# Layer 1's experts hold gate and up weights in the array: products two and four tiles behind the rows, matches in fours

## The reference

```
scores = sigmoid(x @ gate_weight.T)            # 32 experts, biased, in groups; the top 6 of a token
g, u   = x @ w_gate[e], x @ w_up[e]            # 256 -> 128 each, for every chosen expert e
routed = sum over the 6 of  weight * (silu(g) * u) @ w_down[e]
ag, au = x @ anchor_w_gate[l], x @ anchor_w_up[l]   # 256 -> 64 each, one anchor l of 16 per token
anchor = (silu(ag) * au) @ anchor_w_down[l]
x      = x + routed + shared expert + 0.1 * anchor
```

## Time and profile before

| | us |
|---|---|
| median of 3 runs | 1128.87 |
| lowest, highest | 1126.39, 1144.8 |
| the profiled execution's own time | 1131.93 |
| its span, first to last instruction | 1130.2 |
| busy: PE, weight loads, DVE | 943.6, 690.6, 656.6 |
| busy: ACT, POOL | 481.3, 536.7 |

### The profile page before, as it was taken

How to read it: one execution, slowest core, us unless ns; L and a number is a source line. 1 busy time by engine, 2 the same in 40 slices (tenths; PEclk the granted TensorE clock), 3 DMA queues, 4 the chain that set the end, 5 groups by cost and what they waited for, 6 DMA issues and landing times. The chain is left out here.

```text
span 1130.2 us, 23159 instructions
## 1 busy us (share of the span) xinstructions
PE 943.6 (83%) x6360; PEld 690.6 (61%) x6360; DVE 656.6 (58%) x3235; ACT 481.3 (43%) x1594; POOL 536.7 (47%) x543
## 2 busy tenths in 40 slices
PE   5987888765799999969879989758799999998970
PEld 2665665544368889537657657544587777776740
DVE  3676566543135445456877677647465555555578
ACT  2875566443113333226555444221154444454520
POOL 1024555546414444599444344446465555545530
PEclk9998888766799999998987687568899999999965
DMA  9997311003459993465011141276668644444397
GB/s 332 345 371 260 108 59 46 30 10 116 155 172 317 316 317 118 190 237 210 2 67 67 57 174 72 77 290 235 228 206 247 186 144 137 142 136 130 89 366 263
DMA packets 114064, 198.53 MB, mean 176 GB/s; under 512 B 18712, under 2 KB 86381, under 8 KB 110866
## 3 DMA queue, kind: packets, MB, share of 16 engines
q1 hardware_dynamic: 83922, 138.27, 37.4%
q0 software_dynamic: 22944, 50.38, 12.1%
q10 hardware_dynamic: 7072, 8.40, 2.3%
HBM read 113.72 MB, written 98.72 MB: 188 GB/s over the span
## 5 line engine op out<-in xcount | busy, mean ns | idle before, releaser
L986 POOL DMA_INDIRECT buf<-R,RI x240 | 234.9, 979 | 306.5 <-ACT R L1134 158.2
L771 PE MATMUL PS<-R,XT 128*128 x632 | 155.5, 370 | 10.7 <-DVE XT L1598 10.1
L1022 POOL DMA_INDIRECT yb<-YT,DI x98 | 95.3, 973 | 112.8 <-DVE DI L1591 81.0
L315 PE MATMUL PS<-R 128*128 128x256 f32 (+2 forms) x352 | 125.8, 492 | 12.9 <-DMA R<-in_ctxT 10.1
L1598 DVE COPY XT<-PS 128x256 f32<-128x256 f32 x222 | 93.7, 422 | 71.7 <-PE PS L320 53.5
L771 PEld LDWEIGHTS PS<-R,XT 128*128 128x128 f32 x632 | 105.6, 196 | 22.3 <-issue 14.8
L787 PE MATMUL PS<-R,AT 128*128 (+1 forms) x316 | 102.1, 406 | 0.8 <-issue 0.6
L315 PEld LDWEIGHTS PS<-R 128*128 128x128 f32 (+1 forms) x352 | 72.8, 227 | 47.5 <-issue 37.0
L1134 ACT ACTIVATE R<-R,MX 128x120 f32<-128x120 f32 x256 | 80.0, 387 | 33.2 <-DVE MX L1424 21.9
L473 PE MATMUL PS<-C,R 128*120 128x128 f32 x512 | 83.6, 311 | 10.9 <-issue 10.7
L1142 ACT COPY R<-PS 120x512 f32<-120x512 f32 x96 | 54.7, 578 | 87.5 <-PE PS L473 46.3
(11 more groups left out here) (209 smaller groups left out, 1945.8 us busy)
## 6 DMA issues: line engine op xcount, KB each, us to landing
R<-in_ew SPq DMA_DIRECT2D x64, 384.0 KB
BX<-buf SPq DMA_DIRECT2D x128, 140.0 KB
yb<-Z SPq DMA_DIRECT2D x16, 1024.0 KB
R<-yb SPq DMA_DIRECT2D x16, 1024.0 KB, 4.8
R<-buf SPq DMA_DIRECT2D x94, 140.0 KB
R<-in_w SPq DMA_DIRECT2D x8, 1536.0 KB, 11.2
R<-yb SPq DMA_DIRECT2D x8, 1536.0 KB, 10.3
buf<-Z SPq DMA_DIRECT2D x8, 1120.0 KB, 13.5
```

The costliest lines, as they stand in the source:

```text
L315: m = e.matmul(out_, left, right, start=(i == 0), stop=(i == len(pairs) - 1))
L771: x = e.matmul(PS[:, 2 + j % 2, 0:2 * wd], XT[:, j % 3, k, :], src[:, bass.ds(regs[j], 1), k * 2 * wd:(k + 1) * 2 * wd].rearrange("p a n - ...
L986: e.indirect_dma_start(out=(buf1 if l else buf0)[:, :], out_offset=bass.IndirectOffsetOnAxis(ap=RI[:, n % 6, k:k + 1].bitcast(U32), axis=0 ...
L1022: e.indirect_dma_start(out=yb[:, :], out_offset=bass.IndirectOffsetOnAxis(ap=DI[:, j:j + 1].bitcast(U32), axis=0), in_=(YTS0 if i < E0 els ...
```

## The change

For layer 1's experts only:

- PE's gate and up product is turned round. ACT copies a tile's gate and up weights (128x512, or 128x256 for an anchor) from the resident weights, through a register, to one of two halves of `SS_`; PE takes 128x128 pieces of the copy as the stationary operand and streams the turned rows. A routed tile takes four products of 128 columns (each two passes), an anchor tile two, with gate and up side by side in one.
- The product comes out turned, so the transpose of `AC`, the copy to `AT` and their waits are gone; `AC1` (four slots) is the down product's stationary operand.
- The product runs two tiles behind the transposes and the down product four; before they ran one and three behind. Turned rows have three PSUM banks and four slots (`XT1`), products three banks.
- Rows are loaded into 8 slots (`RX`) that lie over H2T, so the first load waits for the last shared product that reads it.
- Matching is done once for four tiles, with four instructions, after all four have landed; a slot's next load waits for its batch. `TE` is written in the order of the tiles for it.
- PE, SP and now ACT load table entries by fours into registers, without the check of their bounds.

```diff
+        h2f = H2T[:, :, :].rearrange("p c n -> p (c n)")
+        RX = h2f[:, 0:NB1 * ROW].rearrange("p (s n) -> p s n", s=NB1)
+        XT1 = h2f[:, 2560:3584].rearrange("p (s c t) -> p s c t", s=4, c=2)
+        AC1 = h2f[:, 3584:4096].rearrange("p (s n) -> p s n", s=4)
+        XB, GB1 = (0, 1, 6), (2, 3, 7)
...
+            def of(self, i):
+                o = ORDER[i]
+                kind, first, size = (0, 0, T1) if o < T1 else (1, T1, TA)
+                b = (o - first) // 4
+                if (kind, b) not in self.had:
+                    at = first + 4 * b
+                    self.had.pop((kind, b - 2), None)
+                    self.had[kind, b] = nc.values_load_multi_w_load_instructions(
+                        self.table[0:1, at:min(at + 4, first + size)], engines=[self.engine], min_val=0,
...
+                return self.had[kind, b][(o - first) % 4]
...
-            for i in range(NTL + 3):
+            who, regs = Numbers(mybir.EngineType.PE, TI, R1 - 1, NA - 1), {}
+            for i in range(NTL + 4):
                 if i < NTL:
-                    regs[i] = e.value_load(TI[0:1, ORDER[i]:ORDER[i] + 1], min_val=0, max_val=(R1 if ORDER[i] < T1 else NA) - 1)
-                    turn_rows(E0 + i)
-                if 0 <= i - 1 < NTL:
...
-                    for k in range(2):
-                        x = e.matmul(PS[:, 2 + j % 2, 0:2 * wd], XT[:, j % 3, k, :],
-                                     src[:, bass.ds(regs[j], 1), k * 2 * wd:(k + 1) * 2 * wd].rearrange("p a n -> p (a n)"),
-                                     start=(k == 0), stop=(k == 1))
-                    x.then_inc(S["s_g"], 1)
+                    w.wait_ge(*landed(i))
+                    if i > 2:
+                        w.wait_ge("d_xt", E0 + i - 2)
+                    tr2(e, PS[:, XB[i % 3], 0:256], RX[:, i % NB1, 0:D]).then_inc(S["s_ta"], 1)
                 if 0 <= i - 2 < NTL:
                     j, wd = i - 2, width(i - 2)
+                    regs[j] = who.of(j)
+                    w.wait_ge("d_xt", E0 + j + 1)
+                    w.wait_ge("a_gu", j + 1)
+                    if j > 2:
+                        w.wait_ge("d_ac", E0 + j - 2)
+                    for o in range(2 if routed(j) else 1):
+                        x = mm(e, PS[:, GB1[j % 3], o * P:o * P + P],
+                               [(SS_[:, j % 2, 2 * wd * k + o * P:2 * wd * k + o * P + P], XT1[:, j % 4, k, :]) for k in range(2)])
+                    x.then_inc(S["s_g"], 1)
+                if 0 <= i - 4 < NTL:
+                    j, wd = i - 4, width(i - 4)
                     w.wait_ge("d_ac", E0 + j + 1)
                     if j > 1:
-                        w.wait_ge("a_at", j - 1)
-                    e.transpose(PS[0:wd, 6 + j % 2, 0:P], AC[:, j % 2, 0:wd], ident).then_inc(S["s_t2"], 1)
...
-                    e.matmul(PS[:, 4 + j % 2, 0:256], AT[0:wd, j % 2, :], src.rearrange("p a n -> p (a n)"),
+                    e.matmul(PS[:, 4 + j % 2, 0:256], AC1[0:wd, j % 4, :], src.rearrange("p a n -> p (a n)"),
                              start=True, stop=True).then_inc(S["s_y"], 1)
...
-                r = e.value_load(TU[0:1, ORDER[i]:ORDER[i] + 1], min_val=0, max_val=DUM_A)
+                r = units.of(i)
+                if i == 0:
+                    w.wait_ge("s_gu", 16 + 4)
...
+                if i >= NB1:
+                    w.wait_ge("s_ta", E0 + i - NB1 + 1)
+                    w.wait_ge("d_m", (i - NB1) // BATCH + 1)
...
+            def gate_copy(j):
+                src = (W1 if routed(j) else WA)[:, bass.ds(who.of(j), 1), 0:4 * width(j)]
+                w.wait_ge(*group_of(j))
+                e.copy(SS_[:, j % 2, 0:4 * width(j)], src.rearrange("p a n -> p (a n)")).then_inc(S["a_gu"], 1)
+
+            for i in range(NTL + 4):
...
+                if 0 <= i - 2 < NTL:
+                    j = i - 2
                     w.wait_ge("s_g", E0 + j + 1)
                     if j > 1:
                         w.wait_ge("d_ac", E0 + j - 1)
-                    e.activation(SL[:, j % 2, 0:wd], PS[:, 2 + j % 2, 0:wd], ACT.Silu).then_inc(S["a_sl"], 1)
...
-                    e.copy(AT[0:wd, j % 2, :], PS[0:wd, 6 + j % 2, 0:P]).then_inc(S["a_at"], 1)
...
+                if 0 <= i - 4 < NTL:
+                    yt_out(E0 + i - 4)
+                if i < NTL:
+                    gate_copy(i)
...
+            def matches1(i):
+
+                n, b = min(BATCH, NTL - i), i // BATCH
+                for k in range(i, i + n):
+                    w.wait_ge(*landed(k))
+                rows = RX[:, i % NB1:i % NB1 + n, :]
+                e.tensor_tensor(MEQ[:, 0:n, :], rows[:, :, 256:264], TE[:, i:i + n].unsqueeze(2).broadcast_to([P, n, 8]),
+                                ALU.is_equal).then_inc(*dv.up())
+                w.wait_ge("dv", dv.n)
+                e.tensor_tensor(MDW[:, 0:n, :, :], rows[:, :, 264:280].rearrange("p j (c k) -> p j c k", c=2),
+                                MEQ[:, 0:n, :].unsqueeze(2).broadcast_to([P, n, 2, 8]), ALU.mult).then_inc(*dv.up())
+                if b > 1:
+                    w.wait_ge("a_yt", E0 + BATCH * (b - 1))
+                w.wait_ge("dv", dv.n)
+                e.tensor_reduce(MS[:, b % 2, 0:n, :], MDW[:, 0:n, :, :], AX.X, ALU.add).then_inc(*dv.up())
+                w.wait_ge("dv", dv.n)
+                e.tensor_scalar(DI[:, i:i + n], MS[:, b % 2, 0:n, 0], OFF, None, ALU.add).then_inc(S["d_m"], 1)
...
+            for i in range(NTL + 4):
                 if i < NTL:
-                    xt_copy(E0 + i)
-                    w.wait_ge(f"bx{(E0 + i) % NBX}", 16 * ((E0 + i) // NBX + 1))
-                    matches(E0 + i, TE[:, ORDER[i]:ORDER[i] + 1])
-                if 0 <= i - 1 < NTL:
...
+                    e.tensor_copy(XT1[:, i % 4, :, :], two(PS[:, XB[i % 3], 0:256])).then_inc(S["d_xt"], 1)
+                    if i % BATCH == 0:
+                        matches1(i)
+                if 0 <= i - 2 < NTL:
+                    j = i - 2
                     w.wait_ge("a_sl", E0 + j + 1)
...
-                if ROUTED + 6 <= i:
-                    yf_add(i - ROUTED - 6)
+                if ROUTED + 7 <= i:
+                    yf_add(i - ROUTED - 7)
```

More of the change, by code:

```diff
@@ L32 @@
 NBX = 7
+NB1 = 8
+BATCH = 4
 NYT = 6
@@ L185, in build @@
         DI = sb("DI", [P, NTL], I32)
-        TE = sb("TE", [P, NTL])
+        TE = sb("TE", [P, NTL + 1])
         TI = sb("TI", [P, NTL], I32)
@@ L341, in all_back, with routed, landed, arrival @@
                 w.wait_ge(f"yt{s}", 16 * n)
+        def routed(i):
+            return ORDER[i] < T1
+        def landed(i):
+            s = i % NB1
+            return arrival(s), 16 * (i // NB1 + 1 + (len(range(s, E0, NBX)) if s < NBX else 0))
+        def arrival(s):
+            return f"bx{s}" if s < NBX else "rx7"
+        def group_of(i):
+            return (f"w1_{min(ORDER[i] // 4, 7)}", 16) if routed(i) else ("wa", 16 * 16)
+        class Numbers:
+            def __init__(self, engine, table, routed_most, anchor_most):
+                self.engine, self.table, self.most, self.had = engine, table, (routed_most, anchor_most), {}
+            def of(self, i):
[7 more added lines that the diff above has]
+                        self.table[0:1, at:min(at + 4, first + size)], engines=[self.engine], min_val=0,
+                        max_val=self.most[kind], skip_runtime_bounds_check_because="the table holds minima with this bound",
+                        bass_reorder=False)[1]
+                return self.had[kind, b][(o - first) % 4]
         def width(i):
@@ L1236, in yt_out @@
                 w.wait_ge("s_y", i + 1)
-                w.wait_ge("d_wc", i + 1)
+                if i < E0:
+                    w.wait_ge("d_wc", i + 1)
+                    weight = WC[:, j % 8:j % 8 + 1]
+                else:
+                    w.wait_ge("d_m", j // BATCH + 1)
+                    weight = MS[:, j // BATCH % 2, j % BATCH, 1:2]
                 slot, n = result(i)
@@ L1242, in yt_out @@
                     w.wait_ge("s_dn", 4 * EARLY if i < E0 else 32)
-                e.activation((YTS0 if i < E0 else YTS)[slot], PS[:, 4 + j % 2, 0:256], ACT.Copy, scale=WC[:, j % 8:j % 8 + 1]).then_inc(
+                e.activation((YTS0 if i < E0 else YTS)[slot], PS[:, 4 + j % 2, 0:256], ACT.Copy, scale=weight).then_inc(
                     S["a_yt"], 1)
@@ L1308, in _ @@
                         w.wait_ge("d_ac", E0 + j - 1)
[L1309 to L1317 removed]
+                    if routed(j):
+                        e.activation(SL[:, j % 2, :], PS[:, GB1[j % 3], 0:P], ACT.Silu).then_inc(S["a_sl"], 1)
+                    else:
+                        e.activation(SL[64:P, j % 2, :], PS[0:64, GB1[j % 3], 0:P], ACT.Silu).then_inc(S["a_sl"], 1)
+                if 0 <= i - 4 < NTL:
+                    yt_out(E0 + i - 4)
+                if i < NTL:
+                    gate_copy(i)
             for g in range(4):
@@ L1893, in _ @@
```

(17 more changed lines are left out.)

75 lines of the change are left out of this document (31 added, 44 removed).

## The result

The changed kernel took 1141.86 us (median of 4 runs, 1136.87 to 1147.64) beside 1133.69 for the kernel before in the same comparison: a ratio of 1.0129, 95% interval 1.0071 to 1.0187. The forecast was 1116 with a range of 1099 to 1139. The time moved the other way, by less than 2%. The profiled execution took 1136.87, its span 1135.2.

The account below looks back on a forecast made before the run. PE's instruction stream was taken to bound layer 1's expert stage, with 24.6 us of stalls besides. Products -10.2, anchors -2.1, start -1.0, drain +1.1 and tail -1.0 sum to -13.2: median some 1116 us, range 1099 to 1139.

Parts of the forecast that it names:

- Stalls: PE's stalls between tiles 3 and 146, 24.6 us before: no net change, 0, with both ends left open.
- over price: Tiles 3 to 146 should take 229.8 us by cost per tile; they took 254.4, the other 24.6 being stalls.
- the copies feel the stalls more: Rival, PE waiting for ACT at the product: some 30 times 0.45 us, +6 to +17 us; 15%.
- Products: PE's routed tiles in layer 1: 0.080 us less than 1.627 each over 127 tiles, -10.2 us.
- anchors: PE's anchor tiles: each loses the 0.11 us transpose, 19 ahead of the last routed tile, -2.1 us.
- The weight-load rule: Rival: four more weight loads lie bare in each routed tile, 4 x 0.196 us a tile, over 1200 us; 2%.
- The copy: ACT's new 128x512 weight copy from SBUF: 0.60 us, starting 1.0 after the product's end, hidden by throughput.
- Its slack: Hand-over of ACT's copy to PE through two buffers: 0.45 us of slack, so hidden.
- Register loads: Loads of four numbers on PE, SP and ACT: 0 taken; four in a row would cost +27 us.
- Start: PE's first transpose no longer waits behind a 0.86 us register load, which comes two tiles later: -1.0 us.
- Drain and tail: Last routed down product one anchor tile later, +1.1 us; four anchor tiles between DVE's final adds, not five, -1.0 us.
- The stalls go: Rival: fewer sequencer instructions and deeper queues remove half to nearly all of 24.6 us, giving 1091 to 1103; 22%.

Follow-up runs that it names:

- before, on time: Kernel before, unedited, in a group where PE's signals are not late: 989.24 us, tiles 3 to 146 in 233.5 us.
- changed, on time: Changed kernel, unedited, against the kernel before where PE's signals are not late: 983.51 us, ratio 0.9944.
- before, late: Kernel before, unedited, in a group where many of PE's signals come over 0.4 us late: 1133.69 us.
- changed, late: Changed kernel, unedited, against the kernel before where many of PE's signals come over 0.4 us late: 1141.86 us, ratio 1.0129.
- the copy ahead: Changed kernel with ACT's weight copy one tile further ahead, three buffers for two; against the kernel before 0.9877 with signals on time, 0.9998 with signals late.
- the two late groups: Unedited changed kernel against the kernel before, twice where PE's signals come late: 1141.86 us (1.0129) and 1137.67 us (1.0054).

## Why the prediction was wrong

Each piece, in us from the end of the table's writes on DVE, forecast beside what the traces show:

| piece | before, on time | changed, on time | forecast | measured | before, late | changed, late |
|---|---|---|---|---|---|---|
| table to tile 3 | 14.9 | 12.5 | -1.0 | -2.4 | 14.1 | 10.7 |
| tile 3 to 146 | 233.5 | 224.7 | -12.3 | -8.8 | 254.4 | 263.6 |
| to the last routed down product | 4.3 | 6.4 | +1.1 | +2.1 | 4.4 | 6.4 |
| to DVE's first sum | 10.6 | 12.6 | 0 | +2.0 | 12.9 | 11.0 |
| first sum to end | 47.6 | 48.5 | -1.0 | +0.9 | 47.5 | 48.6 |
| all | 310.9 | 304.7 | -13.2 | -6.2 | 333.2 | 340.3 |

- **The step that failed: "Stalls. With slack 0.45 for copies and over 2 us for XT and AC, I see no net change", 0.** With late signals the stalls went from 24.6 (over price) to some 44 us (263.6 less the 219.4 that the copy ahead needs on time). That is nearly 20 us against a gain in price of 12, and the whole of the wrong sign. The rival "the copies feel the stalls more" had the place right, PE waiting for ACT ahead of the product, but priced it as 30 events of 0.45 us more. The trace shows both terms wrong: each stall costs 1.2 us, and Silu is answered late 43 times, not 22. I had taken the number of late signals as given by the machine. It isn't: it grew with the change, while the price of one stayed at 0.9 to 1.0 us. The times say the same: the change gains 5.7 us by the medians on time and loses 8.2 and 2.7 in the two late groups.
- **Why it grew is not settled.** Excluded by a run: the rows that the write-backs move. The copy's short slack explains where PE stops, not how often signals are late: with more slack there were still 37 late answers. In the changed kernel PE starts twelve matmuls and twelve weight loads in 1.546 us, where the kernel before had nine in 1.627, and its sequencer no longer loads a number in every tile. Neither was tested on late signals. But density alone doesn't do it: in layer 0's experts PE starts the same twelve in 1.55 us, and there 4 of 143 signals are over 0.4 us late in the late trace of the kernel before and 5 of 144 in the changed kernel's, against 94 of 414 and 130 of 341 between tiles 3 and 146 of layer 1; its down products follow each other by 1.55, 1.55 and 3.26 us there, late or on time.
- *Products, -10.2 and anchors, -2.1: right.* 1.546 a tile. Four routed tiles and an anchor take 8.08 us before and 7.62 with the copy ahead, where nothing waits (7.78 in the changed kernel): 0.46 less, forecast 4 x 0.080 + 0.11 = 0.43. On time the stretch of the copy ahead is 14.1 us under that of the kernel before, which itself stood 3.7 over its price of 229.8.
- *The weight-load rule* of the Trainium skill ("TensorE: Matmul & The Clock Gate", section "The mechanism"), that a load overlaps only where the row group differs, predicts bare loads. Eight loads run within 0.89 us of eight matmuls here too, so the measurement decides against it for this form. (The same section of the Trainium skill also excepts loads that go to the background weight buffer; which kind these are, no run shows.)
- *The copy: right in size*, 0.62 us (0.60 taken), start and end within 0.1 us. *Its slack: right for routed tiles, wrong after an anchor*, which shortens the round to 1.10 us: 5.3 us, and visible only where signals are on time. I had priced the anchor as a gain and not as a shorter cover.
- *Register loads, 0: right.* On ACT's sequencer four by one instruction took 0.316 us, the median on time, where one alone took 0.284: near a round trip, as the prediction had it, and hardly a count of words. The 200 ns a register of the Trainium skill ("Runtime: NRT & Kernel Launch", section "Instruction fetch mechanics") would give 0.8 by estimate; the trace is lower.
- *Start: mis-sized.* The first transpose comes 1.5 us sooner behind the tables on time (7.53 in place of 9.04), and tiles 0 to 3 follow in 4.9 in place of 5.9: -2.4 in place of -1.0.
- *Drain and tail: mis-sized.* Down now stands four tiles behind the rows, in place of three, and the tiles there are an anchor and slow iterations: +2.1. DVE's sums set the end, and its anchor tiles between them did not get cheaper: +0.9 in place of -1.0. The matches in fours are worth 2.8 there, so something else of the new order costs it; which, no run shows. The 2.0 us before the first sum are within what other traces of both kernels show (10.6 to 12.9).
- *"The stalls go"* (22%) was the worst of the rivals: fewer sequencer instructions and deeper queues did not calm the signals.
- PE's own work on the anchor tiles behind the last routed one is not on the path in either kernel: the sums on DVE begin some 19 us before PE is done.

The copy one tile ahead is the version to keep. On time it is 0.9877 and 0.9853 of the kernel before and faster than the changed kernel; with late signals it is level with the kernel before (0.9998, 0.9950 to 1.0046) and 0.6% under the changed one, which the overlapping intervals leave open.

## What to carry to other kernels

A stall that comes from outside the kernel's own arithmetic must not be carried over as a constant: ask how often its cause fires and not only what each one costs, and time a change under both conditions before judging it. Count the slack of a ring of two buffers over its shortest round, not its usual one. Where more slack on one hand-over brings little, look at which wait ends last next; here it went from the copy to the bank of the down product.

## What the runs showed of the hardware

- The same kernel took 989 to 994 us in some groups and 1120 to 1135 in others. In the stage of the change the durations of instructions are equal and the granted clock is 1.00 in both traces of the kernel before; there the difference is that signals of PE come late. Over the whole late trace it is a fifth of PE's recorded signals that come over 0.4 us late (455 us of lateness summed), over half of them in bursts of three to seven within 0.5 us. No recorded signal of ACT was late. Ahead of tile 3 the clock is lower as well, at half for 252 us against 92. "Late" is counted from the end of the matmul in the trace, which is modelled, and more signals are missing from the late traces (1140 of 1414 recorded, against 1393), so the trace can't tell a signal that was held from work that ended later than modelled.
- The late signals are not spread evenly over the kernel: 4 of 143 in layer 0's experts and 94 of 414 between tiles 3 and 146 of layer 1, in the same trace. What makes the difference was not tested.
- After PE had stood idle for 3.25 us the granted clock was 0.5, 1.2 GHz, for 3.4 us, and eight matmuls took 2.04 us in place of 1.06.
- One load of four numbers took 316 ns on ACT's sequencer, the median of 40 in the changed kernel on time (304 to 925), one of a single number 284 (median of 158 in the kernel that loads by one, 272 to 980). On PE's sequencer the medians are 366 and 306.
